# A two-layer transformer kernel on one core: the second list of expert tiles in pairs and half tiles, their rows stored in place, and the order of work searched anew

## The reference, cut to what matters

```python
scores = jax.nn.sigmoid(xf @ gate_w + bias)
top_scores, top_idx = jax.lax.top_k(scores, K)              # K = 2 of E = 8
top_scores = top_scores / (jnp.sum(top_scores, axis=-1, keepdims=True) + 1e-06)
w = jnp.zeros((T, E), dtype=xf.dtype).at[jnp.arange(T)[:, None], top_idx].add(top_scores)
up = jnp.einsum('th,ehi->tei', xf, up_w) + up_b              # 128 -> 512
hact = jax.nn.gelu(up, approximate=False)
eo = jnp.einsum('tei,eih->teh', hact, down_w) + down_b       # 512 -> 128
combined = jnp.einsum('teh,te->th', eo * 0.1, w)
shared = (jax.nn.gelu(xf @ sw_up + sb_up, approximate=False) @ sw_down + sb_down) * 0.1
out = (shared + combined).reshape(b, s, h)
out = out / (jnp.max(jnp.abs(out), axis=-1, keepdims=True) + 1e-06)
```

## Time and profile before

| | us |
|---|---|
| median of three runs | 765.45 |
| the three runs | 763.49, 765.45, 765.53 |
| the profiled execution | 762.66 |
| its span on the engines | 760.9 |
| attention and routing | 0 to 334 |
| between, the shared expert and first fetches | 334 to 347 |
| first list, 17 tiles | 347 to 424 |
| second list, 22 tiles | 424 to 507 |
| gathers and layer 1 | 507 to 761 |
| mean granted clock of TensorE | 0.978 of full |

### The profile page before, as it was taken

The page is one execution under the profiler, slowest core; times in us unless marked ns, Lnnn a source line. Parts: engine busy times, 40 slices in busy tenths (PEclk is TensorE's granted clock), DMA queues, the critical chain, the costliest instruction groups (busy, mean ns, idle before and its releaser), DMA issues.

```text
span 760.9 us, 12350 instructions
## 1 busy us (share of the span) xinstructions
PE 696.3 (92%) x3608; PEld 424.0 (56%) x3608; DVE 505.9 (66%) x1906; ACT 481.8 (63%) x734; POOL 388.6 (51%) x562
## 2 busy tenths in 40 slices
PE   4999999999997999887999699996999999999994
PEld 4544444545444544347988699984655544444442
DVE  2598879989998899973452244422345678795572
ACT  2767687677784767565544355552587959777553
POOL 7427354656776667742422255534455575722253
PEclk9999999999999999998999899999899999999998
DMA  9992000000000000028676688811010101000002
GB/s 273 380 383 70 1 1 0 9 15 15 19 19 16 14 15 22 22 84 236 193 203 206 192 249 245 243 51 32 28 29 24 33 23 40 25 4 0 0 15 83
DMA packets 65597, 66.79 MB, mean 88 GB/s; under 512 B 7105, under 2 KB 48410, under 8 KB 65530
## 3 DMA queue, kind: packets, MB, share of 16 engines
q1 hardware_dynamic: 59152, 52.46, 22.8%
q0 software_dynamic: 6320, 13.53, 5.6%
q10 hardware_dynamic: 58, 0.02, 0.0%
HBM read 37.80 MB, written 28.18 MB: 87 GB/s over the span
## 4 chain that ended last, share of the span: by engine, by line
PE 56%; DVE 22%; issue 7%; ACT 5%; DMA 4%; SPq 2%; POOL 2%; DVEq 0%; ACTq 0%; POOLq 0%
PE PS L1085 9%; DVE JK L1271 8%; PE PS L948 4%; PE PS L1135 3%; PE PS L891 3%; PE PS L986 3%; PE PS L1066 3%; PE PS L1149 3%; PE PS L1142 3%; PE PS L897 2%; PE PS L903 2%; PE PS L988 2%; PE PS L911 1%; DMA got<-expert_out,IG 1%; PE PS L1072 1%
## 5 line engine op out<-in xcount | busy, mean ns | idle before, releaser
L1271 DVE CUSTOM_DVE_ANT_0 JK<-PS,CM 128x256 bf16<-128x256 f32 (+1 forms) x512 | 149.1, 351 | 7.0 <-PE PS L948 5.7
L1763 ACT ACTIVATE GF<-PS,XN 128x256 f32<-128x256 f32 x156 | 73.5, 475 | 72.9 <-PE PS L1074 41.6
L948 PE MATMUL PS<-KZ,QS 128*128 128x512 f32 x192 | 88.4, 497 | 7.8 <-DVE MX L1271 5.6
L1085 PE MATMUL PS<-WD,GF 128*128 128x128 f32 x624 | 94.0, 276 | 0.0
L1941 POOL DMA_INDIRECT got<-expert_out,IG x64 | 64.5, 1007 | 50.3 <-DMA got<-expert_out,IG 33.1
L1085 PEld LDWEIGHTS PS<-WD,GF 128*128 128x128 f32 x624 | 86.4, 193 | 2.8
L1913 POOL DMA_INDIRECT expert_rows<-five,IU x64 | 63.3, 990 | 32.5 <-DMA expert_rows<-five,IU 14.9
L1724 ACT ACTIVATE PA<-PS 128x1024 f32<-128x1024 f32 x64 | 64.7, 1026 | 15.2 <-PE PS L971 14.1
L1863 POOL TENSOR_SCALAR H<-xc,MOD 128x256 f32<-128x256 f32 x56 | 33.3, 603 | 68.0 <-DVE xc L1240 60.8
L1900 POOL TENSOR_SCALAR_AFFINE_SELECT PA<-PA 128x256 f32<-128x256 f32 x128 | 49.8, 419 | 27.9 <-ACT PA L1724 27.3
L1924 POOL DMA_DIRECT2D expert_out<-YT x39 | 21.7, 558 | 80.3 <-DVE YT L1523 80.3
(11 more groups left out here) (289 smaller groups left out, 1710.1 us busy)
## 6 DMA issues: line engine op xcount, KB each, us to landing
expert_rows<-five SPq DMA_DIRECT2D x16, 1024.0 KB, 12.6
WU<-in_L_ffn_up_w SPq DMA_DIRECT2D x39, 256.0 KB, 3.2
WD<-in_L_ffn_down_w SPq DMA_DIRECT2D x39, 256.0 KB, 3.4
XT<-expert_rows SPq DMA_DIRECT2D x39, 128.0 KB, 3.7
expert_out<-YT POOLq DMA_DIRECT2D x39, 128.0 KB, 3.4
BD<-in_L_ffn_down_b SPq DMA_DIRECT2D x39, 64.0 KB, 3.3
PA<-in_L_attn_x SPq DMA_DIRECT2D x8, 256.0 KB, 5.5
out<-yo SPq DMA_DIRECT2D x8, 256.0 KB, 2.4
```

The costliest lines, as they stand in the source:

```text
L948: pe.matmul(bk.rearrange("p (j n) -> p j n", n=wd), q, ks, start=True, stop=True).then_inc(sems["mx_mm"], 1)
L1085: m = pe.matmul(bk[:, b], g[:, b], wd[:, k, :], start=(k == 0 and t == 0), stop=(k == 3 and t == blocks - 1))
L1271: m = dve.tensor_tensor_reduce(JK[n % 2][:, s], bk[:, s], CM[:, 256 - wd:256] if wd == 128 else CM[:, 0:256], -1.0, 3.0e38, ALU.add, ALU.m ...
L1763: act.activation(GF[slot["gf", kind, u, k]][:, 0:n], bank("up", kind, u, k)[:, 0:n], ACT.Gelu, bias=bias).then_inc(sems["gelu"], 1)
```

## The change

Eight edits go together.

- The second list takes 15 tiles of 256 rows (17 to 31; `NP` = 32) and seven of 128 rows (32 to 38), `rows(t)`. `plan_halves` counts, for each expert, whole pairs of half tiles and at most one single half tile that is left. A half tile is fetched with one block of rows, transposed once, and goes through plain fp32 up matmuls of 128 columns and single down matmuls; its weights aren't split.
- An expert's results are stored into `expert_rows`, at the rows from which the tile was read, which POOL reads from `EI` into a register before each store. `expert_out`, `IG` and the part of `plan_rows` that made it are gone; the gathers use the scatter's indices `IU`. `EI` gets a place of its own, and `expert_rows` 256 more rows with a zeroing DMA on SP.
- The scatter's and gather's semaphores alternate with k. A gather of the first chunk waits for the last but one; the others for the one before.
- The planner's costs are given anew (some are shown), a step of attention now has a form for its row half, with a turn cost of -0.213 where a step of the other half is beside it; landings are stages of their own ("spread", "got_in").
- `ORDER1` and `ORDER2` are other tables.

```diff
@@ -26,14 +26,22 @@
...
+NP = NT - E + 1
+M2 = NT - N1
+HALF = 128
...
+NSEL = S_CAP + M2
...
+def rows(t):
+    return TR if t < NP else HALF
...
@@ -88,7 +97,7 @@
...
-    "gather": ("POOL", 2.35, None), "cmb": ("DVE", 2.25, None), "fin1": ("DVE", 1.94, None), "fin2": ("PE", 0.436, None),
+    "spread": ("DMA", 0.0, None), "got_in": ("DMA", 0.0, None), "gather": ("POOL", 2.3, None), "cmb": ("DVE", 2.25, None), "fin1": ("DVE", 1.94, None), "fin2": ("PE", 0.436, None),
...
@@ -100,12 +109,11 @@
...
-FORM = {"atm": 1, "pv": 2}
-TURNS = ((0.0, 0.1, 0.1), (0.2, 0.0, 0.2), (0.1, 0.1, 0.0))
-NARROW = {"dpm": 0.06, "rtm": 0.05, "vm": 0.15, "modmm": 0.2}
-HOPS = {"PE": 0.06, "ACT": 0.035, "DVE": 0.035, "POOL": 0.085, "SP": 0.03}
-BEHIND = {"PE": 0.25, "ACT": 0.12, "DVE": 0.08, "POOL": 0.045, "SP": 0.0}
-LANDS = {"gather": 2.5, "scatter": 2.5, "fetch": 3.0}
+TURNS = ((0.0, 0.11, 0.11, 0.1), (0.21, 0.115, -0.213, 0.21), (0.21, -0.213, 0.115, 0.21), (0.12, 0.12, 0.12, 0.01))
+NARROW = {"dpm": 0.06, "rtm": 0.05, "vm": 0.15, "modmm": 0.2, "atm": 0.11, "mxm": 0.213}
+HOPS = {"PE": 0.06, "ACT": 0.035, "DVE": 0.035, "POOL": 0.085, "SP": 0.03, "DMA": 0.0}
+BEHIND = {"PE": 0.25, "ACT": 0.12, "DVE": 0.08, "POOL": 0.045, "SP": 0.0, "DMA": 1.65}
+LANDS = {"fetch": 3.0, "store": 2.0}
...
@@ -123,52 +131,57 @@
+def form_of(name, key):
+    return 1 + key[1] % 2 if name == "atm" else 3 if name == "pv" else 0
...
-    "AFAAAAAAAAABAGAGABACAAAAAAABADABAEABABABAAAAAGAGAHAHAAAAAAAKAKAGAGAGABABALALANANAGANANAMAMAMAMAJABABAJABAHAHAPAPAQAQAOAO"
...
+    "AFAAAAACABAAAGABABAAABAGAAAAAAADAEABABABAAAAAGAGAKAKAAAAAAALALAGAGABABAHAHAGAGANANANANAGAMAMAMAMABABABAJAJAHAHAPAPATATAQ"
...
@@ -427,10 +440,14 @@
...
-        yield stage("htt", c, takes=[(RR, "ht", (c,), ("ht", c))], after=[("ln_mod", c, "f0")] + ([("scatter", c - 2, k) for k in range(4)] if c > 1 else []))
+        yield stage("htt", c, takes=[(RR, "ht", (c,), ("ht", c))], after=[("ln_mod", c, "f0")] + ([("spread", c - 2, k) for k in range(4)] if c > 1 else []))
...
-            yield stage("scatter", c, k, after=[("dpd", c)] + ([("scatter", c - 1, 3)] if c and not k else []))
+            n = 4 * c + k
+            yield stage("scatter", c, k, after=[("dpd", c)] + [("spread", (n - 1) // 4, (n - 1) % 4)] * (n > 0))
+
+    def lands(name, of, c, k):
+        yield stage(name, c, k, after=[(of, c, k)])
...
@@ -520,6 +537,8 @@
...
     def weights_in(t):
+        if t >= NP:
+            return
...
@@ -558,8 +577,11 @@
...
-            yield stage("gather", c, k, takes=[] if k else [(GOT, "got", (c,), ("cmb", c))], after=[("gather", c - 1, 3)] if c and not k else [])
-        yield stage("cmb", c, after=[("ev", "s", c)])
+            n = 4 * c + k
+            yield stage("gather", c, k, takes=[] if k else [(GOT, "got", (c,), ("cmb", c))],
+                        after=[("gather", (n - 1) // 4, (n - 1) % 4)] * (n > 0)
+                        + [("got_in", (n - m) // 4, (n - m) % 4) for m in [1 if c else 2] if n >= m])
+        yield stage("cmb", c, after=[("ev", "s", c)] + [("got_in", c, k) for k in range(4)])
...
@@ -1048,7 +1069,7 @@
...
-            for k in range(TB):
+            for k in range(rows(t) // 128):
...
@@ -1062,8 +1083,9 @@
...
-                if u < N1:
-                    pe.matmul(bk[:, 0:TR], WU[u % NF][:, f], XS[slot["xs", u]][:, :], start=True, stop=True).then_inc(sems["up"], 1)
+                if not N1 <= u < NP:
+                    pe.matmul(bk[:, 0:rows(u)], WU[u % NF][:, f], XS[slot["xs", u]][:, 0:rows(u)], start=True, stop=True
+                              ).then_inc(sems["up"], 1)
...
@@ -1377,114 +1399,135 @@
...
+        def plan_halves():
+            left, late, cnt, pairs, odd = p8[6:11]
+            total = p8[11][:, 0:1]
+            base, first, step, count = p16
+            le, lp, t0, t1, half = LE2[:, :, :], LP2[:, :, :], *(x[:, :] for x in pt)
+            w.wait_ge(*at("dp_ix", NCH - 1))
+            w.wait_ge(own_dve, done[0])
+            dve.memset(le[:, :, 16:17], 0.0)
+            t = own(dve.tensor_tensor(left, RUN[:, NCH - 1], base[:, 0:8], ALU.subtract))
+            w.wait_ge(*t)
+            own(dve.tensor_scalar(late, left, -float(HALF), None, ALU.add))
+            t = own(dve.tensor_tensor(p64[0], left.unsqueeze(2).to_broadcast([128, 8, T // TR]),
...
+            w.wait_ge(*t)
+            dve.tensor_scalar(EI[:, 1, N1:NT], t1, float(E * CAP), None, ALU.min).then_inc(sems["pl_ei"], 1)
 
...
         def plan_rows():
-            own(dve.tensor_tensor(a, sl, off, ALU.subtract))
-            t = own(dve.tensor_tensor(b, sl, lim, ALU.is_ge))
-            t = own(dve.tensor_tensor(b, b, gap, ALU.mult))
-            t = own(dve.tensor_tensor(a, a, b, ALU.add))
-            t = own(dve.tensor_tensor(a4, a4, mask, ALU.mult))
-            own(dve.tensor_reduce(hi32[:, :], a, AX.X, ALU.max))
-            t = own(dve.tensor_reduce(sum32[:, :], a, AX.X, ALU.add))
-            dve.tensor_copy(IG[:, 0, :], hi32[:, :])
-            dve.tensor_tensor(IG[:, 1, :], sum32[:, :], hi32[:, :], ALU.subtract).then_inc(sems["pl_ix"], 1)
+            t = own(dve.tensor_tensor(a.rearrange("p (c k) e -> p c k e", k=4), sl, mask, ALU.mult))
+            t = own(dve.tensor_reduce(hi32[:, :], a, AX.X, ALU.max))
             t = own(dve.tensor_tensor(b, a, hi32[:, :].unsqueeze(2).to_broadcast([128, NCH * 4, 8]), ALU.is_equal))
...
@@ -1904,14 +1948,12 @@
...
-            w.wait_ge(zero_rows, 16 * 16)
-            if k:
-                w.wait_ge(scattered[c % 2], 128 * (c // 2) + 32 * k)
-            elif c:
-                w.wait_ge(scattered[(c - 1) % 2], 128 * ((c - 1) // 2 + 1))
+            w.wait_ge(zero_rows, 16 * 17)
+            if c or k:
+                w.wait_ge(scattered[(k - 1) % 2], 64 * c + 32 * ((k + 1) // 2))
...
-                                        in_=HT[c % 2][:, k, :], in_offset=None).then_inc(scattered[c % 2], 16)
+                                        in_=HT[c % 2][:, k, :], in_offset=None).then_inc(scattered[k % 2], 16)
...
@@ -1921,7 +1963,9 @@
...
-            pool.dma_start(YD[TR * t:TR * t + TR, :].rearrange("(p k) d -> p (k d)", k=TB), YT[t % 3][:, :]
+            n = rows(t)
+            row = pool.value_load(EI[0:1, 1, t:t + 1], min_val=0, max_val=E * CAP)
+            pool.dma_start(XD[bass.ds(row, n), :].rearrange("(p k) d -> p (k d)", k=n // 128), YT[t % 3][:, 0:n]
...
@@ -1929,18 +1973,16 @@
...
-                w.wait_ge(*at("pl_ix"))
...
-                if c:
-                    w.wait_ge(*got_ready(c - 1))
-            else:
-                sem_, all_ = got_ready(c)
-                w.wait_ge(sem_, all_ - 128 + 32 * k)
+            if c:
+                w.wait_ge(gathered[(k - 1) % 2], 64 * c + 32 * ((k + 1) // 2))
+            elif k > 1:
+                w.wait_ge(gathered[k % 2], 32 * (k // 2))
...
-                pool.indirect_dma_start(out=got[b][n][:, k, :], out_offset=None, in_=YD[:, :],
-                                        in_offset=bass.IndirectOffsetOnAxis(ap=IG[:, n, 4 * c + k:4 * c + k + 1], axis=0)
-                                        ).then_inc(gathered[b], 16)
+                pool.indirect_dma_start(out=got[b][n][:, k, :], out_offset=None, in_=XD[:, :],
+                                        in_offset=bass.IndirectOffsetOnAxis(ap=IU[:, c, n, k:k + 1], axis=0)
+                                        ).then_inc(gathered[k % 2], 16)
...
@@ -1996,6 +2038,7 @@
...
+        sp.dma_start(XD[E * CAP:E * CAP + TR].rearrange("(p r) d -> p (r d)", r=2), ZT[:, 0:2 * D]).then_inc(zero_rows, 16)
...
@@ -2017,15 +2060,16 @@
...
-            row = sp.value_load(EI[0:1, 1, t:t + 1], min_val=0, max_val=E * CAP - TR)
+            n = rows(t)
+            row = sp.value_load(EI[0:1, 1, t:t + 1], min_val=0, max_val=E * CAP)
...
-            for n in range(2):
-                w.wait_ge(scattered[n], 128 * len(range(n, NCH if t >= N1 else C1, 2)))
-            sp.dma_start(XT[k][:, :, :], XD[bass.ds(row, TR), :].rearrange("(p k) d -> p k d", k=TB)).then_inc(ld_t[k], 16)
+            w.for_all((landed, 64 * (NCH if t >= N1 else C1)) for landed in scattered)
+            sp.dma_start(XT[k][:, 0:n // 128, :], XD[bass.ds(row, n), :].rearrange("(p k) d -> p k d", k=n // 128)
+                         ).then_inc(ld_t[k], 16)
...
```

286 lines of the change are left out of this document (151 added, 135 removed).

## The result

| | us |
|---|---|
| after, median of 20 runs (768.91 to 776.50) | 771.45 |
| before, median of 20 runs (763.49 to 773.70) | 767.29 |
| ratio after to before, 95% interval | 1.0052 (1.0033 to 1.0072) |
| after, the profiled execution; its span | 771.74; 770.1 |

A forecast was written before the change was run, and what follows sets the result against it. PE, busy 92% of the 760.9 us span, was taken to bound the kernel. The terms summed to +0.5 us on a profiled 762.66, thus 763.2; allowing for the runs' higher median gave 765.0 us, range 757.5 to 772.5.

The forecast's parts named there:

- 1 half tiles: Second list: seven half tiles at 1.87 us instead of pairs at 3.42 save 10.9, less 1.6 for a late fetch: -9.3 us.
- 2 fetch of tile 18: Hand-over between the lists: tile 18's fetch moves to the end of its group on SP, so PE waits longer: +9.6 us.
- 3 start of the first list: First list's start: fetch 0 now precedes ten late loads on SP, so the gates land 3.2 us later: +2.7 us.
- 4 attention: Attention: 31 couples of overlapping steps instead of 17 save PE 5.9 us, DVE takes back about half: -3 us.
- 5 plans, in the first list: DVE beside PE's first list: the second list's plan grows while plan_rows loses six of fifteen instructions: +0.5 us.
- 6 POOL's load: Before each store on POOL: a register load, taken at 0.55 us, fits in 1.56 us of slack: 0.
- 7 gathers and tail: After the lists: gathers end some 5 us earlier, but shared experts' groups moved behind keep PE's idle near 7 us: 0.
- (d): Rival, slower: in the second list the feed or lag bounds the halves, -9.3 shrinks to about -3, 771 us; chance 0.12.
- (b): Rival, slower: POOL's register load costs over 1.56 us and sets the pair tiles' pace, 776.7 at 2.0 us; chance 0.07.
- (c): Rival, slower: one more DVE and POOL port lock stall in attention costs 4 us, 769; chance 0.09.
- (a): Rival, faster: halves, attention and tail give all, the start costs at most 2: 756.7, more likely 759 to 761; chance 0.34.

The follow-up runs named there:

- b_sorted: The kernel before with only SP's fetches put in the order of the tiles: 761.73 us, ratio 0.9879 to the kernel before.
- a_sorted: The changed kernel with only SP's fetches put in the order of the tiles: 759.85 us, ratio 0.9863 to the kernel before.
- a_late_first: The changed kernel with SP issuing layer 1's ten late loads before the fetch of tile 0: 770.27 us, ratio 0.9987 to the kernel before.
- a_serial: The changed kernel with each gather of the first chunk waiting for the one before: 776.45 us, ratio 1.0111 to the kernel before.
- a_pool5: The changed kernel with four more register loads before each store on POOL: 798.67 us, ratio 1.0427 to the kernel before.

## Why the prediction was wrong, point by point

The forecast was 765.0 us and no measurable change; the kernel became 0.5% slower. Term by term, with the stretches' means over the profiles that have the same code in a stretch:

| term | forecast | measured |
|---|---|---|
| 1 half tiles | -9.3 | -6.8 |
| 2 fetch of tile 18 | +9.6 | +10 (+9.3 in the first two profiles) |
| 3 start of the first list | +2.7 | +2.7 |
| 4 attention | -3.0 | -1.2 |
| 5 plans, in the first list | +0.5 | +2.4 |
| 6 POOL's load | 0 | 0 |
| 7 gathers and tail | 0 | 0 |
| sum | +0.5 | +7.1 by stretches, +4.2 by medians |

The stretches give 3 us more than the medians do. b_sorted shows the same sign: its profile says 3.7 us and its runs 7.6. Both would follow if unprofiled executions of the kernel before are some 3 us longer than its profiles say; what that would be isn't known, and attention's spread of 5 us can hold it too. So the terms are known from the profiles to a few microseconds, not better.

- **Fetch order (2): right**, by mechanism and size. It was the largest loss; a_sorted takes it back.
- **Start (3): right** in size, half of it by luck. The late loads were the wait, and a_late_first gives it back and more. But PE's idle time grew only from 4.85 to 6.12 us, not to 7.5; the rest is that the shared block and the router's part took 3.27 us at half clock, where 1.66 had been put.
- **Gathers and tail (7): right**, and a_serial shows the 4.6 us that the term set against the moved groups.
- **POOL's load (6): right** in sign, wrong in price: 0.90 us, not 0.55, still under the 1.56 of slack. a_pool5 shows the loss beyond it.
- **Half tiles (1): the step that failed is "only one fetch still has to start".** The count was of fetches that wait for a half tile's YT. But SP issues one fetch in 3.2 us or more, and the halves take 1.9, so the fetches that wait for the last pairs are late too: that of tile 37 starts at 501.97, 2.7 us behind tile 31's YT, and tile 38's at 506.28. The halves' own price was right: with two transfers a fetch the list is 10.6 us shorter than before, where 10.9 was said. The feed costs 3.8 to 4.1 us, where 1.6 was taken, so the term lacked 2.5. The rival (d) had this, at a price of 6.
- **Attention (4): the step that failed is "DVE takes back about half".** PE's steps did take 5.1 us less, near the 5.9 that was said. PE's own other work took most of it back (the statistics of the layer norms and fills, which the prediction put at nothing), while PE's idle time stayed; no more than about 1 us is left. Why the statistics take longer in the new order isn't known. The lock cost 3.03 us of PE in the new order at another place and 3.84 in the old: that they swap was foreseen, their size too.
- **Plans (5):** the first list takes 64.7 to 66.1 us in the new order (leaving out a_pool5) and 62.9 to 63.7 in the old. That the plan on DVE does it isn't shown, and the profiles speak against it. From before to after PE's own time in the list grew from 61.6 to 62.6 us and its idle time from 2.2 to 3.2; of that, waits for DVE went from 1.3 to 1.0 and waits for ACT from 0.3 to 1.5. The term lacked what the list's new order does on PE and ACT; which part of the order isn't known, and no run here separates it.
- **The base.** All terms came from one execution that was 7 us faster, ahead of the expert lists, than the next one. This didn't enter the sum, but the median of three did, 765.45 where that of 20 is 767.29. Of the 6.5 us between 765.0 and 771.45, 2.8 are the base's and 3.7 the sum's (+4.2 for +0.5).

Three terms (1, 4 and 5) missed by 1.8 to 2.5 us each, all to the slower side, and that made a change that can be measured out of a forecast of none. The range, 757.5 to 772.5, holds the median of 771.45. Of the rivals, (d) came true in its mechanism, (b) and (c) didn't. The time that (a) named, 759 to 761, came only once the fetch order was repaired (a_sorted, 759.85), and not by (a)'s terms, of which neither the whole of the halves nor attention's 6 us came.

## What to carry to other kernels

When an order is searched anew, read each queue that the search doesn't price: here both losses, PE's idle times of 11.4 us (3.2 before) and 6.1 (4.85 in two before), sat in SP's queue, where a transfer wanted soon stood behind others wanted late. A few lines took back 17 us, part of which the kernel before had been losing too. Work cut in halves needs a feed that is cut too; where each fetch has a fixed issue time, the time per fetch against the time per tile tells how many in a row can be small. And price from two profiles of the kernel before if there are two, since a few microseconds of one may be that execution's own.

## What the runs showed of the hardware

TensorE's granted clock falls to half, 1.2 of 2.4 GHz, for some microseconds at places that can move from one execution to the next. Windows of 20 us in attention (us, busy us of PE, PEld, DVE, ACT, POOL, granted clock, DMA), in after and then in a_late_first, whose attention is the same code:

```profile
20.00:40.00 20.00, 18.52 (x65) 9.97 (x65) 7.76 (x23) 13.74 (x24) 6.87 (x10) 0.83 1.04 381
160.00:180.00 20.00, 16.89 (x92) 8.26 (x91) 17.00 (x72) 12.37 (x19) 10.69 (x19) 1.00 0.05 17
```

```profile
20.00:40.00 20.00, 17.33 (x70) 9.51 (x69) 7.62 (x22) 13.97 (x24) 5.89 (x9) 1.00 1.03 381
160.00:180.00 20.00, 16.82 (x90) 8.78 (x89) 16.55 (x70) 9.49 (x15) 11.52 (x20) 0.83 0.06 20
```

The granted clock is 0.83 and 1.00 in one, 1.00 and 0.83 in the other, with PE busy for 17 to 18.5 of the 20 us in each. In the 16 profiles attention had 3.4 to 17.1 us at half clock.

- A DVE instruction on 16 x 128 elements takes 0.2 to 0.4 us or 2.0 to 2.4, at the same place, by the execution.
- Two attention steps of 32 rows take 0.43 us side by side in opposite row halves and 0.66 in the same rows.
- POOL's masks cost attention 10.5 us in the profiles of both kernels, of which the long DVE instructions (4.25 and 3.21 us) are a part; DVE's busy time falls by 12.4 and 13.6 us with short masks, its instructions being the same.
- A register load on POOL costs 0.90 us on the way from YT to the store, and some 0.56 for each further one.
